# State-space stage: GpSimd adds the squares of C between the two halves of the decays

## What is computed

```python
Bm = rmsnorm(Bm, Bn_w) + B_bias          # x @ WB.T, (batch, length, 64 heads, 128)
Cm = rmsnorm(Cm, Cn_w) + C_bias
theta_cumsum = jnp.cumsum(theta * dt[..., None], axis=1)
Bm = rope(Bm, theta_cumsum)
Cm = rope(Cm, theta_cumsum)
alpha = jnp.exp(dt * A)
# for each token t:
h = at * h + bt * outer(B_prev, x_prev) + gt * outer(Bt, xt)
yt = Ct . h
```

## Time and profile before

| | us |
|---|---|
| median of 3 runs | 7745.34 (7743.88 to 7745.35) |
| profiled execution | 7747.07 |
| its span, first to last instruction | 7745.3 |
| mean granted TensorE clock | 0.863 of full speed |
| PE busy | 6985.7 (90%) |
| DVE busy | 4741.5 (61%) |
| ACT busy | 3713.1 (48%) |
| POOL busy | 3482.4 (45%) |

### The profile page before, as it was taken

How to read it: one execution, slowest core, us unless ns; L and a number is a source line. 1 busy time by engine, 2 the same in 40 slices (tenths; PEclk the granted TensorE clock), 3 DMA queues, 4 the chain that set the end, 5 groups by cost and what they waited for, 6 DMA issues and landing times. The chain is left out here.

```text
span 7745.3 us, 137299 instructions
## 1 busy us (share of the span) xinstructions
PE 6985.7 (90%) x43387; PEld 5087.3 (66%) x43660; DVE 4741.5 (61%) x8121; ACT 3713.1 (48%) x5855; POOL 3482.4 (45%) x3893
## 2 busy tenths in 40 slices
PE   6999999999684699999999999999999999997499
PEld 4777777777573566666666666666666666666287
DVE  4333333333555477777777777777777777772433
ACT  2222222222222366666666666666666666662111
POOL 0000000000000477777777777777777777771000
PEclk8555555555796899999999999999999999998699
DMA  1000000000101211111111111111111111112100
GB/s 47 4 9 1 4 9 4 9 4 1 57 22 49 89 27 29 28 27 27 28 29 27 30 27 27 29 27 30 27 28 27 27 29 29 29 27 95 53 22 16
DMA packets 388293, 214.26 MB, mean 28 GB/s; under 512 B 248036, under 2 KB 343076, under 8 KB 387140
## 3 DMA queue, kind: packets, MB, share of 16 engines
q1 hardware_dynamic: 379588, 203.05, 10.1%
q10 hardware_dynamic: 8448, 8.39, 0.3%
HBM read 162.02 MB, written 40.64 MB: 26 GB/s over the span
## 5 line engine op out<-in xcount | busy, mean ns | idle before, releaser
L1117 POOL MEMSET ss_rot<- 128x4096 f32 x1 | 3.5, 3511 | 2500.9 <-POOLq L1815 2500.9
L1350 ACT ACTIVATE ss_r<-ss_pssum,ss_eps 128x512 f32<-128x512 f32 x512 | 352.5, 688 | 1131.1 <-PE ss_pssum L1280 1131.1
L1280 PE MATMUL ss_pssum<-ss_sq,ss_pairssum 128*128 128x512 f32 x1024 | 595.4, 664 | 184.0 <-POOL ss_sq L1171 181.2
L1159 POOL TENSOR_TENSOR ss_sq<-ss_sq 128x512 f32<-128x512 f32 x256 | 329.6, 1288 | 914.9 <-ACT ss_sq L1359 914.9
L1409 DVE SCALAR_TENSOR_TENSOR ss_psb<-ss_psb,ss_norm,ss_r 128x512 f32<-128x512 f32 x512 | 362.9, 755 | 510.3 <-ACT ss_r L1352 510.3
L329 PE MATMUL a_ps_o<-a_probt,a_vhead 128*128 128x128 f32 x2560 | 639.7, 414 | 3.6 <-issue 3.5
L329 PEld LDWEIGHTS a_ps_o<-a_probt,a_vhead 128*128 128x128 f32 x2560 | 604.5, 330 | 4.0 <-ACT a_probt L383 1.6
L1261 PE MATMUL ss_psse<-ss_rot 64*128 64x128 f32 x8224 | 530.0, 279 | 0.3 <-POOL ss_rot L1144 0.3
L427 DVE TENSOR_REDUCE a_nmax<-a_ps_p 128x1 f32<-128x384 f32 (+1 forms) x256 | 159.9, 625 | 598.7 <-PE a_ps_p L305 598.7
L1192 POOL TENSOR_TENSOR ss_own<-ident,ss_tk 128x512 f32<-128x512 f32 x512 | 524.9, 1048 | 0.0
L48 PE MATMUL ss_psb<-x_hi,ss_whi 128*128 x1024 | 515.3, 503 | 6.7 <-DVE ss_fr L1397 4.5
(11 more groups left out here) (339 smaller groups left out, 18260.8 us busy)
## 6 DMA issues: line engine op xcount, KB each, us to landing
ss_dtb<-time_steps SPq DMA_DIRECT2D x516, 128.0 KB, 2.9
ss_wraw<-in_w_state SPq DMA_DIRECT2D x264, 80.0 KB, 2.4
ss_xp<-x_heads SPq DMA_DIRECT2D x33, 256.0 KB, 4.4
y_heads<-ss_yo SPq DMA_DIRECT2D x132, 64.0 KB, 2.4
x_heads<-xp_outt SPq DMA_DIRECT2D x32, 256.0 KB, 2.0
ss_right<-decay_rows SPq DMA_DIRECT2D x512, 3.0 KB
ss_left<-decay_rows SPq DMA_DIRECT2D x512, 3.0 KB
op_y<-y_heads SPq DMA_DIRECT2D x8, 1024.0 KB, 6.8
```

Source lines behind the costliest of these rows:

```text
L1159: G.tensor_tensor(sq[:, 0, 0], sq[:, 0, 0], sq[:, 0, 1], ALU.add).then_inc(ss_b, 1)
L1280: M(p_sum[:], pairs_sum[:], sq[:, q, 0], start=True, stop=True).then_inc((sum_b, sum_c)[q], 1)
L1350: A(r[:, q], p_sum[:], ACT.Ln, scale=1.0 / N1, bias=eps[:, 0:1]).then_inc(ln, 1)
```

## The change

POOL's addition of the squares of C (with its wait for ACT's squares, `sq_c`) moves from behind both halves of the decays to between them. The arithmetic is the same. The last call of `decays`, after the loop, has no squares to add, hence the new argument.

```diff
-            def decays(k):
+            def decays(k, squares_c):
                 pool.wait_ge(d_done, k + 1)
                 pool.wait_ge(own_done, k)
                 G.tensor_tensor(dec[:, 0:TPB], dec[:, 0:TPB], own[:, 0:TPB], ALU.add)
+                if squares_c:
+                    pool.wait_ge(sq_c, k + 1)
+                    G.tensor_tensor(sq[:, 1, 0], sq[:, 1, 0], sq[:, 1, 1], ALU.add).then_inc(ss_c, 1)
                 G.tensor_tensor(dec[:, TPB:2 * TPB], dec[:, TPB:2 * TPB], own[:, TPB:2 * TPB], ALU.add).then_inc(dd_done, 1)
...
-                    decays(k)
-
-                    pool.wait_ge(sq_c, k + 1)
-                    G.tensor_tensor(sq[:, 1, 0], sq[:, 1, 0], sq[:, 1, 1], ALU.add).then_inc(ss_c, 1)
+                    decays(k, True)
...
-            decays(UNITS)
+            decays(UNITS, False)
```

## The result

The changed kernel takes 7558.96 us (median of 4 runs, 7553.5 to 7561.0), the kernel before, run beside it, 7745.35: ratio 0.9758, 95% interval 0.9741 to 0.9775. That is 186 us less, where 131 were forecast (7614, range 7595 to 7665). The direction and the mechanism held, the size didn't.

A forecast was written before the change was run, and what follows sets the result against it. The prediction took the 17.00 us circle over ACT, POOL and PE as the bound: 7747.1 - 122 (DVE's slack) - 9 (clock falls) = 7616, with the median 1.7 lower, so 7614 us; range 7595 to 7665.

The forecast's parts named there:

- POOL's circle of 17.00 us: Loop from ACT's logarithm for C through POOL's sum of C's squares and PE back to ACT; claimed to set the turn.
- The turn can follow only to DVE's circle: With POOL's loop cut by 1.23 to 15.77 us, DVE's loop was to limit the gain to about 0.44 us a turn.
- DVE's circle is 16.62 or 16.50: Loop from DVE's rotation of C through `fr`, rotation of B, states and mask: 6.51 + 3.46 + 5.51 + 1.14 us, by parity.
- through PE and ACT to the rotation of B at 4514.22 (3.46): Part of DVE's loop from the start of `fr` to the rotation of B, put at 3.46 us.
- falls of the clock: 20 turns of 17.94 us for 17.00, PE's squares of C taking 2.07 us for 1.13 at the lower clock level.
- DVE's slack: DVE's wait for r of C in front of the rotation of C, about 0.44 us a turn, taken as the gain.
- Slack in front of the rotation of C, 122 us: DVE's idle time there over all turns, 103.7 us, plus 18 us for starting 0.08 us sooner; all to be gained.
- The falls go, 9 of 11 us: Slow-clock turns behind PE's wait for POOL's sum of C cost 11 us beyond the slack; 9 taken as gained.
- The rule on transposes: Transposes don't count as PE activity like matmuls, so slow-clock stretches might move to B's squares; chance 0.10, or 0.04 for slower.
- The four covers: Added waits: POOL for ACT's squares of C 0.1 to 0.3 us; PE covered by 0.6, mask 1.1, rotated B/`own` 3.42.
- The wait for ACT's squares of C: New wait of POOL in front of its moved sum of C's squares, put at 0.1 to 0.3 us.
- The bounds: Main case: 7592 if all 11 us go and r of B comes 0.08 sooner; 7634 if falls stay, DVE loses 0.04.

The follow-up runs named there:

- squares_first: The changed kernel with POOL's sum of C's squares moved once more, in front of both halves of the decays: 7642.6 us.

## Why the prediction was right and wrong

- *POOL's circle of 17.00 us sets the turn*: right. Two edits on it, on POOL and on ACT, gave the same 187 us; edits of 0.60 us more and about 0.7 us less on DVE gave nothing.
- *The turn can follow only to DVE's circle*: right. The turn is DVE's circle to 0.01 us, and 0.60 us more on DVE cost 0.60.
- *DVE's circle is 16.62 or 16.50*: the step that failed. In "through PE and ACT to the rotation of B at 4514.22 (3.46)" I took a measured distance for a fixed one. It holds a wait for POOL's sum of B, that is for the circle that the change shortens; free of it the step is 3.29, and DVE's circle closes at 16.33. In the mean over the turns of the stage the step fell from 3.53 to 3.29, by 0.24 us, of which falls of the clock account for 0.05. 0.19 x 256 = 49 of the 55 us missing. So DVE's slack was 0.67 us a turn and not 0.44.
- *Slack in front of the rotation of C, 122 us*: right. Mask to rotation fell from 1.61 to 1.13 in the mean, 0.48 x 256 = 123.
- *The falls go, 9 of 11 us*: right, and all of them went: PEclk is 1.00 and no squares of 2.07 us are left. The rule on transposes (the Trainium skill, "TensorE: Matmul & The Clock Gate", Part 4) gave a fear that didn't come true: PE's weight load for the squares of B now stands idle 0.55 us in every turn, and no fall shows. But the prediction overlooked the tiny matmuls (L1249), which stand between the transposes and that wait, so the rule is neither borne out nor refuted here.
- *The four covers*: all held. The wait for ACT's squares of C was 0.15 (0.1 to 0.3), the mask doesn't wait for the decays. squares_first shows that one more add uses that cover up. PE's own stream, and not POOL's sum of C, still decides when the squares of C start: the sum starts 1.76 us before them, where it was 1.32.
- *The bounds*: 7592 allowed 0.08 us a turn on this step. The rows gave a sign of more: PE starts 0.05 us after POOL's sum of C ends (4517.38 + 1.27 = 4518.65, start 4518.70), but 0.22 after `fr` (4510.76 + 0.69 = 4511.45, start 4511.67). `fr` was named as the releaser and wasn't the last; POOL's sum of B ended at 4510.23 + 1.29 = 4511.52. The bound put the 0.08 down to PE standing ready; measured, the step gave 0.19 besides the falls.

## What to carry to other kernels

In this loop with engines in step, the time was the longest circle of waits, not the busiest engine; follow each until it closes, and an edit gains the distance to the next circle. Before calling a step of the next circle fixed, look at every hand-over in it: where the start comes later after the named releaser's end than at other hand-overs, another one, perhaps on the circle that is about to shrink, may have been last, and the step will shrink too (here 0.13 us and more against 0.05). One kernel with a dose on the next circle, below and above its supposed slack, measures that slack for the price of one run.

## What the runs showed of the hardware

A DVE copy of 128 x 512 between two SBUF tiles, 417 ns at its shortest, took 1104 to 1232 ns in the changed kernel. The timelines of DVE and POOL there: the copy begins under a running GpSimd add, ends 0.29 us after that add's end, and GpSimd's next pair of products takes 2.23 us for the usual 2.04.

```profile
4509.39 1.22 DVE L1447 COPY ss_pad<-ss_ones 128x512 f32<-128x512 f32 x1
```

```profile
4509.02 1.30 POOL L1188 TENSOR_TENSOR ss_rot<-ss_rot,ss_tmp 128x512 f32<-128x512 f32 x1
4510.29 2.23 POOL L1193 TENSOR_TENSOR ss_own<-ident,ss_tk 128x512 f32<-128x512 f32 x2
```

It is so in all 256 turns of both kernels with the copy, the shortest one of 417 ns included: the copy begins under that add (L1188) and ends 0.3 us after it. So this copy seems to wait for the GpSimd instruction to end; no run has it with GpSimd idle, and its time alone isn't known. The half product of the mask, which reads one operand from PSUM, takes 0.60 us a turn in the changed kernel and in the one before, each time but the last under a GpSimd instruction; its own duration, 0.68 us, is the same in that last turn, where GpSimd is idle. The Trainium skill ("GPSIMD Engine Reference", section 1, Specifications) says that GpSimd shares its SBUF interfaces with VectorE, and names DVE instructions in a 2-port mode or with two SBUF inputs as those that meet it; the trace agrees in that the copy met GpSimd and took up to 0.7 us longer than its shortest, and the half product, with one SBUF input, didn't. Whether the copy ran in a 2-port mode no run shows.
